# Block diagonals written by ScalarE, the input norm ahead of its slot, and new orders of the units for all rounds but the first four

## The chip, the cores and the metric

One core of a Trainium2 chip runs the kernel; the other cores are idle. The metric is the device time of one execution in microseconds. The median of 3 runs of the kernel before is 1451.22 us (1449.34 to 1452.15).

## What is computed

The input `x` is 128 entries of 32 rows of 512 numbers, with a context of 257 rows for each entry. Three residual layers follow each other, each behind a plain layer norm. Shortened:

```python
x = x + xattn(norm(x), ctx)     # causal self attention (1 head, mask inside an entry), layer norm with gamma, beta;
                                # attention over the entry's 257 context rows, layer norm;
                                # relu(h @ W1 + b1) + h, layer norm, relu
x = x + attn(norm(x))           # 16 heads of 32: q, k, v = x @ W_attn; causal softmax, times a decay matrix; @ W_proj
x = x + ffn(norm(x))            # silu(x @ w1 + b1) * (x @ w2 + b2), layer norm, @ w3 + b3;
                                # the rows named by an index list get gated outputs of 8 experts added
```

Everything is f32 outside; the large products are made of f16 parts.

## The kernel before

The 4096 rows are 32 tiles of 128 rows (4 entries each). A tile passes through some forty units (a unit is a few instructions of one engine: `turn_xn` on TensorE transposes the normed input, `turn_xn` on ScalarE copies it out of PSUM as f16, and so on). Three tiles are in work at once, in three slots (`SLOTN`, tile mod 3), whose buffers and PSUM banks `ps_t[s]` and `ps_a[s]` all units of the tile share; slot 2's buffers lie in one tensor, `last_slot`.

Nothing is scheduled at run time. For each engine a table names the units of one round in order, each with a lag: `(2, "project_k")` in round n is done for tile n - 2. `FIRST` holds for rounds 0 to 3 (with the set-up of the weights, `set_...`), `ORDER` for rounds 4 to 29, `LAST` from round 30 on (with the units of the experts for one tile, `e_...`); `run_pipeline` walks the tables. After the rounds a hardware loop does the expert passes. Between engines there are semaphores only, so an engine stands still when the first instruction of its next unit is not ready, whatever stands behind it.

A product of an activation with a weight has this path: the rows are transposed by TensorE (`turn_...`, four 128x128 f32 transposes), ScalarE copies the result as f16 (`act_h`, the unit of the same name) and once more as f32 (`act_t`, the unit with `_t`), GpSimd makes the remainder `act_l` = `act_t` - `act_h`, TensorE multiplies `act_h` with both parts of the weight (`project_...`, `hidden`, `ffn_in`) and then `act_l` with the high part (the unit with `_l`). Layer norms are on VectorE: `bn_stats`, `bn_aggr`, an addition (`moments`), then GpSimd raises the variance to -0.5 (line 636), then VectorE scales.

The parts that the change touches:
- Lines 1200 and on: `xn_moments` and `turn_xn` (function `xn`) norm the tile's input; they use the slot's `stats`, `mv`, `var` and `rstd`, which the slot's other norms use too.
- Self attention: `self_scores` (VectorE, line 1206) adds the mask, takes the row maximum and scales it into `ntop`; ScalarE exponentiates; `turn_p` transposes the 128x128 weights on TensorE into `ps_a` (line 1770) and ScalarE copies them to `p_t` (line 826); `self_mix` multiplies them with the values.
- Heads: the keys of the 16 heads are laid out block diagonally in `kbd`, so that a matmul serves four heads: `project_k` writes two 32-partition blocks on ScalarE (line 850) and two on VectorE (line 1309). The softmax weights are put block diagonally into `pbd`: `head_weights` on VectorE scales and then transposes four groups of 32 partitions into it (line 1349). TensorE's `head_scores` (line 1814) and `head_mix` (line 1826) read `kbd` and `pbd` as moving operands of 128 columns.
- `ffn_out` on VectorE (lines 1389 and 1391) scales the product and adds `b3`, then adds the residual.
- `Chain` (VectorE): each step of a chain is followed by a wait for its own end.

```python
kbd = of_arena(HALF + 5 * C * D + 16, C * G * HPC * T).rearrange("p (c g h k) -> p c g h k", c=C, g=G, h=HPC)
pbd = of_arena(HALF + 6 * C * D + 16, NH * G * T).rearrange("p (h g q) -> p h g q", h=NH, g=G)
```

## Time and profile before

| | us |
|---|---|
| median of 3 runs | 1451.22 (1449.34 to 1452.15) |
| span of the profiled execution | 1452.8 |
| TensorE (PE) busy | 1365.6, 94% |
| VectorE (DVE) busy | 1128.1, 78% |
| ScalarE (ACT) busy | 601.9, 41% |
| GpSimd (POOL) busy | 526.1, 36% |

The profiled execution is one more execution of the kernel, and all rows below are of it. A matmul's busy time reaches to its modelled end, which lies behind the start of the next; the time that a unit takes in TensorE's queue is read from start to start. PEld is the loading of weights into TensorE, which goes on beside the matmuls. In the lists of instructions a bracket gives the idle time of the engine before the row and what ended it.

### The profile page before, as it was taken

The page shows a single profiled execution, that of the slowest core. Times are in us where ns is not written, and L with a number is a line of the kernel's source. Part 1 is how long each engine was busy: PE and PEld are TensorE (multiplying, and loading weights), DVE is VectorE, ACT ScalarE, POOL GpSimd, SP SyncE. Part 2 cuts the span into 40 slices and gives each one's busy share as a digit, 9 for nine tenths or more (in the row PEclk, how much of TensorE's full clock was granted, in tenths as well). Part 3 has the DMA queues.
Part 4 walks back from the last instruction along what each step waited for, and adds up shares of the span by engine and source line. Part 5 has one row for each costly group of instructions (what it writes and reads, how often), then busy time and mean ns, then how long its engine had stood idle before and what let it go on. Part 6 is the DMA issues. An engine that isn't in the chain of part 4 may idle for free.

```text
span 1452.8 us, 33270 instructions
## 1 busy us (share of the span) xinstructions
PE 1365.6 (94%) x13860; PEld 851.7 (59%) x13861; DVE 1128.1 (78%) x2335; ACT 601.9 (41%) x1147; POOL 526.1 (36%) x545
## 2 busy tenths in 40 slices
PE   7679999999999999999999999999999999998888
PEld 3355566666656666665665656666665666655443
DVE  6787777777787877778778877777778877777776
ACT  2544444443444444343434444444444444443222
POOL 0133333433444333443443333343443433343222
PEclk9899999999999999999999999999999999999899
DMA  9732444433333444433333344443333344434440
GB/s 349 259 131 74 146 146 146 144 123 105 133 112 115 146 146 146 146 137 101 122 130 105 139 146 146 146 142 114 111 138 105 123 146 146 147 134 161 149 161 30
DMA packets 38662, 201.41 MB, mean 139 GB/s; under 512 B 5096, under 2 KB 5992, under 8 KB 28400
## 3 DMA queue, kind: packets, MB, share of 16 engines
q1 hardware_dynamic: 37648, 198.93, 38.3%
q8 instruction: 109, 1.79, 0.5%
q10 hardware_dynamic: 864, 0.36, 0.1%
q14 instruction: 41, 0.34, 0.1%
HBM read 182.24 MB, written 17.04 MB: 137 GB/s over the span
## 4 chain that ended last, share of the span: by engine, by line
PE 70%; DVE 19%; POOL 4%; ACT 4%; issue 3%; DMA 0%; DVEq 0%; POOLq 0%; ACTq 0%; SPq 0%
PE ps_a L1716 11%; PE ps_a L1739 8%; PE ps_t L1739 7%; PE ps_t L1703 6%; PE ps_a L1725 6%; PE ps_a L1751 4%; PE ps_a L1783 4%; POOL rstd L636 4%; PE ps_t L1716 3%; PE ps_v L1716 3%; DVE stats L1178 3%; DVE arena L1309 3%; PE ps_t L1826 2%; PE ps_t L1775 2%; PE ps_t L1751 2%
## 5 line engine op out<-in xcount | busy, mean ns | idle before, releaser
L645 POOL TENSOR_TENSOR act_l<-act_t,act_h 128x512 f16<-128x512 f32 (+1 forms) x176 | 199.5, 1134 | 351.4 <-ACT act_t L789 199.4
L636 POOL TENSOR_TENSOR rstd<-var,mhalf 128x1 f32<-128x1 f32 x224 | 181.8, 812 | 333.7 <-DVE var L1180 328.9
L781 ACT ACTIVATE act_h<-ps_t,scale 128x512 f16<-128x512 f32 (+1 forms) x110 | 70.8, 644 | 206.2 <-PE ps_t L1703 206.2
L645 POOL TENSOR_TENSOR last_slot<-last_slot 128x512 f16<-128x512 f32 x80 | 90.0, 1125 | 156.7 <-ACT last_slot L789 90.8
L1739 PE MATMUL ps_a<-act_h,arena 128*128 128x128 f16 x1408 | 87.6, 221 | 17.3 <-ACT act_h L781 17.3
L1739 PEld LDWEIGHTS ps_a<-act_h,arena 128*128 128x128 f16 x1408 | 81.9, 99 | 28.3 <-ACT act_h L781 21.3
L789 ACT ACTIVATE act_t<-ps_t,scale 128x512 f32<-128x512 f32 (+1 forms) x110 | 70.3, 639 | 49.1 <-PE ps_t L1703 49.1
L1739 PE MATMUL ps_t<-act_h,arena 128*128 128x128 f16 x1408 | 87.0, 221 | 3.3 <-ACT act_h L781 3.3
L1716 PE MATMUL ps_a<-arena,act_h 128*128 128x512 f16 x352 | 83.6, 380 | 1.9 <-ACT act_h L781 1.9
L1309 DVE TENSOR_SCALAR arena<-ps_a,unscale 32x512 f32<-32x512 f32 x64 | 48.2, 753 | 47.0 <-PE ps_a L1751 45.8
L1739 PEld LDWEIGHTS ps_t<-act_h,arena 128*128 128x128 f16 x1408 | 81.4, 99 | 4.9 <-DVE arena L1037 2.4
L1178 DVE BATCH_NORM_STATS2 stats<-rows 128x6 f32<-128x512 f32 x110 | 76.5, 695 | 3.8
L781 ACT ACTIVATE last_slot<-ps_t,scale 128x512 f16<-128x512 f32 (+1 forms) x50 | 32.2, 644 | 89.4 <-PE ps_t L1703 89.4
L1191 DVE SCALAR_TENSOR_TENSOR rows<-rows,rstd,beta 128x512 f32<-128x512 f32 x66 | 50.2, 761 | 22.3 <-POOL rstd L636 22.2
L1716 PE MATMUL ps_a<-w_parts,act_h 128*128 128x512 f16 x264 | 64.2, 379 | 2.0 <-ACT act_h L781 2.0
L1703 PE MATMUL ps_t<-ident,rows 128*128 128x128 f32 x352 | 56.1, 283 | 9.1 <-DVE rows L1184 7.4
L1349 DVE STREAM_TRANSPOSE arena<-rows 32x512 f32<-32x512 f32 x88 | 61.8, 703 | 2.8
L1799 PE MATMUL ps_a<-arena,p_t 128*32 128x512 f32 x512 | 62.6, 607 | 0.0
L1716 PEld LDWEIGHTS ps_a<-arena,act_h 128*128 128x128 f16 x352 | 31.3, 98 | 50.6 <-ACT act_h L781 10.5
L1703 PEld LDWEIGHTS ps_t<-ident,rows 128*128 128x128 f32 x352 | 41.0, 143 | 29.0 <-DVE rows L1184 20.1
L1187 DVE SCALAR_TENSOR_TENSOR rows<-rows,mv,gamma 128x512 f32<-128x512 f32 x66 | 50.3, 762 | 0.0
L1783 PE MATMUL ps_a<-arena,q_t 128*32 128x257 f32 x704 | 44.2, 393 | 4.7 <-ACT q_t L830 4.7
(380 smaller groups left out, 3150.7 us busy)
## 6 DMA issues: line engine op xcount, KB each, us to landing
arena<-in_ctx_t SPq DMA_DIRECT2D x32, 2056.0 KB, 8.4
arena<-in_ctx_n SPq DMA_DIRECT2D x32, 2048.0 KB
ctx_last<-in_ctx_last SPq DMA_DIRECT2D x32, 256.0 KB
arena<-in_ew SPq DMA_DIRECT2D x8, 1024.0 KB, 6.3
x_in<-in_x SPq DMA_DIRECT2D x22, 256.0 KB, 7.3
x_scratch<-rows SPq DMA_DIRECT2D x22, 256.0 KB, 8.8
out<-rows SPq DMA_DIRECT2D x22, 256.0 KB, 2.1
arena<-in_ew SPq DMA_DIRECT2D x8, 512.0 KB, 7.2
```

Of the source, the lines that this page charges most:

```text
L636: nc.gpsimd.tensor_tensor(rstd[s][:], var[s][:], mhalf[:], ALU.pow).then_inc(rstd_ready[s], 1)
L645: nc.gpsimd.tensor_tensor(act_l[s][:, chunks], act_t[s][:, chunks], act_h[s][:, chunks], ALU.subtract).then_inc(act_l_ready[s], 1)
L781: nc.scalar.activation(act_h[s][:, 0:width // P].rearrange("p c r -> p (c r)"), bank[s][:, 0:width], ACT.Copy, scale=scale[:, k:k + 1]).th ...
L789: nc.scalar.activation(act_t[s][:, 0:width // P].rearrange("p c r -> p (c r)"), bank[s][:, 0:width], ACT.Copy, scale=scale[:, k:k + 1]).th ...
L1178: chain(nc.vector.bn_stats(stats[s][:], rows))
L1309: nc.vector.tensor_scalar(kbd[rows, :, :, h, :], ps_a[s][rows, :].rearrange("p (c g k) -> p c g k", c=C, g=G), unscale[rows, K_WATTN:K_WAT ...
L1703: mm = nc.tensor.transpose(out[s][:, c * P:(c + 1) * P], rows[s][:, lo + c * P:lo + (c + 1) * P], ident[:])
L1716: nc.tensor.matmul(bank[s][:], act_h[s][:, c, :], w[:, part, c, lo:lo + D], start=(c == 0 and part == 0), stop=False, skip_group_check=True)
L1725: mm = nc.tensor.matmul(bank[s][:], act_l[s][:, c, :], w[:, 0, c, lo:lo + D], start=False, stop=(c == chunks - 1), skip_group_check=True)
L1739: nc.tensor.matmul(bank[s][:, m * P:(m + 1) * P], w[:, part, c, lo + m * P:lo + (m + 1) * P], act_h[s][:, c, :], start=(m == 0 and c == 0 ...
L1751: mm = nc.tensor.matmul(bank[s][:, m * P:(m + 1) * P], w[:, 0, c, lo + m * P:lo + (m + 1) * P], act_l[s][:, c, :], start=False, stop=(c == ...
L1783: mm = nc.tensor.matmul(ps_a[s][T * g:T * (g + 1), 0:S], q_t[s][:, c, T * g:T * (g + 1)], ctx_t[:, c, g, :], start=(c == 0), stop=(c == C ...
```

## The change

- `kbd` and `pbd` get another order of their axes: the four heads (or groups) of a moving operand no longer lie side by side but 512 words apart, while what is written per head or group is one contiguous piece of 512 words.
- All four key blocks are written by ScalarE, in two units (`project_k`, `project_k2`). VectorE's `project_k` is gone.
- `head_weights` on VectorE does one transposing operation of full width; four copies on ScalarE (`heads_p`, `heads_p2`) put the groups into `pbd`.
- `turn_p` is one block transpose on VectorE (the weights are block diagonal in blocks of 32) in place of TensorE's transpose and ScalarE's copy.
- `b3` is added to the residual by GpSimd (`x2_bias`); `ffn_out` is one operation.
- The input norm has its own small buffers and semaphores (`x_stats`, `x_mv`, `x_var`, `x_rstd`), so that it can be done while the slot still serves tile n - 3. `turn_xn` on VectorE waits for the slot's `turn_x2n`, and TensorE's `project_self` waits for `out_ready` of that tile.
- The scale of the scores is folded into constants; the row maxima are taken negated, so that the one-column scaling after them goes.
- The last step of a chain is not waited for at once, but by its next user (`made_by`).
- `ORDER` and `LAST` are new tables. In `LAST` most units have a lag higher by one, which shifts where its round begins. `FIRST` keeps its sequence, with the units that are gone taken out and the new ones put in.

The core of the diff; `LAST` and `FIRST`, semaphore declarations and renumbered waits are left out:

```diff
 ORDER = {
-    "pe": [(2, "project_q"), (3, "turn_z"), (2, "project_k_l"), (3, "ffn_out"), (3, "ffn_out_l"), (1, "turn_pc"),
-        (2, "project_q_l"), (1, "context_mix"), (2, "head_scores"), (0, "turn_xn"), (2, "project_v"),
-        (0, "project_self"), (0, "project_self_l"), (1, "turn_w"), (2, "project_v_l"), (1, "context_out"),
-        (0, "self_scores"), (1, "context_out_l"), (0, "value_self"), (0, "value_self_l"), (0, "turn_p"),
-        (2, "head_mix"), (0, "self_mix"), (2, "project_out"), (1, "turn_h2"), (2, "project_out_l"), (1, "hidden"),
-        (1, "hidden_l"), (0, "turn_h"), (2, "turn_x2n"), (0, "project_query"), (0, "project_query_l"), (2, "ffn_in"),
-        (0, "context_scores"), (2, "ffn_in_l"), (1, "turn_x1n"), (1, "project_k")],
-    "dve": [(3, "z_norm"), (2, "project_k"), (3, "ffn_out"), (0, "xn_moments"), (1, "context_total"), (0, "turn_xn"),
-        (2, "head_scores"), (1, "context_mix"), (1, "context_scaled"), (2, "head_total"), (0, "project_self"),
-        (2, "head_weights"), (0, "self_scores"), (1, "context_out"), (1, "context_norm"), (0, "self_mix"),
-        (2, "project_out"), (0, "self_norm"), (2, "x2_norm"), (1, "hidden"), (1, "out_norm"), (1, "x1_norm"),
-        (2, "ffn_in"), (0, "context_scores"), (2, "silu")],
-    "act": [(3, "turn_x2n_t"), (2, "turn_x1n"), (3, "ffn_in"), (2, "turn_x1n_t"), (3, "turn_z"), (3, "turn_z_t"),
-        (1, "context_scores"), (2, "project_k"), (1, "turn_pc"), (2, "project_q"), (0, "turn_xn_t"), (0, "turn_xn"),
-        (1, "context_sum"), (2, "head_scores"), (1, "context_scaled"), (0, "project_self"), (1, "turn_w"),
-        (1, "turn_w_t"), (0, "self_scores"), (2, "project_v"), (0, "value_self"), (0, "turn_p"), (2, "head_mix"),
-        (2, "head_mix_t"), (1, "turn_h2"), (1, "turn_h2_t"), (0, "turn_h"), (0, "turn_h_t"), (2, "turn_x2n"),
-        (0, "project_query")],
-    "pool": [(3, "silu"), (3, "turn_z"), (0, "xn_moments"), (0, "turn_xn"), (2, "head_scores"), (1, "turn_w"),
-        (1, "context_out"), (2, "head_mix"), (0, "self_mix"), (1, "turn_h2"), (2, "project_out"), (0, "turn_h"),
-        (1, "hidden"), (2, "turn_x2n"), (1, "out_norm"), (1, "turn_x1n")],
+    "pe": [(2, "project_v"), (1, "turn_pc"), (2, "project_q"), (3, "turn_z"), (2, "project_k_l"), (1, "context_mix"),
+        (2, "project_q_l"), (3, "ffn_out"), (3, "ffn_out_l"), (0, "turn_xn"), (2, "head_scores"),
+        (2, "project_v_l"), (1, "turn_w"), (0, "project_self"), (0, "project_self_l"), (1, "context_out"),
+        (1, "context_out_l"), (0, "value_self"), (0, "self_scores"), (0, "value_self_l"), (2, "head_mix"),
+        (1, "turn_h2"), (0, "self_mix"), (2, "project_out"), (2, "project_out_l"), (1, "hidden"), (0, "turn_h"),
+        (1, "hidden_l"), (0, "project_query"), (0, "project_query_l"), (2, "turn_x2n"), (0, "context_scores"),
+        (2, "ffn_in"), (1, "turn_x1n"), (2, "ffn_in_l"), (1, "project_k")],
+    "dve": [(0, "xn_moments"), (3, "ffn_in"), (3, "silu"), (3, "z_norm"), (1, "context_total"), (0, "turn_xn"),
+        (1, "context_mix"), (1, "context_scaled"), (3, "ffn_out"), (2, "head_scores"), (2, "head_total"),
+        (0, "project_self"), (2, "head_weights"), (1, "context_out"), (0, "self_scores"), (1, "context_norm"),
+        (0, "turn_p"), (0, "self_mix"), (0, "self_norm"), (2, "project_out"), (1, "hidden"), (2, "x2_norm"),
+        (1, "out_norm"), (1, "x1_norm"), (0, "context_scores")],
+    "act": [(2, "turn_h2"), (2, "turn_h2_t"), (1, "turn_h_t"), (1, "turn_h"), (1, "project_query"), (3, "turn_x2n"),
+        (3, "turn_x2n_t"), (2, "turn_x1n"), (3, "ffn_in"), (2, "turn_x1n_t"), (1, "context_scores"),
+        (1, "turn_pc"), (3, "turn_z_t"), (2, "project_k2"), (3, "turn_z"), (2, "project_k"), (2, "project_q"),
+        (1, "context_sum"), (1, "context_scaled"), (0, "turn_xn_t"), (0, "turn_xn"), (2, "head_scores"),
+        (1, "turn_w_t"), (1, "turn_w"), (0, "project_self"), (2, "heads_p"), (2, "project_v"), (2, "heads_p2"),
+        (0, "self_scores"), (0, "value_self"), (2, "head_mix"), (2, "head_mix_t")],
+    "pool": [(2, "turn_x1n"), (0, "xn_moments"), (3, "turn_z"), (3, "x2_bias"), (0, "turn_xn"), (2, "head_scores"),
+        (1, "turn_w"), (1, "context_out"), (2, "head_mix"), (0, "self_mix"), (1, "turn_h2"), (2, "project_out"),
+        (0, "turn_h"), (1, "hidden"), (1, "out_norm"), (2, "turn_x2n"), (2, "silu")],
 }
...
-            kbd = of_arena(HALF + 5 * C * D + 16, C * G * HPC * T).rearrange("p (c g h k) -> p c g h k", c=C, g=G, h=HPC)
-            pbd = of_arena(HALF + 6 * C * D + 16, NH * G * T).rearrange("p (h g q) -> p h g q", h=NH, g=G)
+            kbd = of_arena(HALF + 5 * C * D + 16, C * G * HPC * T).rearrange("p (h c g k) -> p h c g k", c=C, g=G, h=HPC)
+            pbd = of_arena(HALF + 6 * C * D + 16, NH * G * T).rearrange("p (g h q) -> p g h q", h=NH, g=G)
...
+                def x2_bias(s, r, tile):
+                    pool.wait_ge(rows_ready[s], 5 * r + 4)
+                    pool.wait_ge(x2_stored[s], 16 * r + 32)
+                    if tile == 0:
+                        pool.wait_ge(late_loaded, 16 * 7)
+                    nc.gpsimd.tensor_tensor(rows3[s][:], rows3[s][:], b3[:], ALU.add).then_inc(x2_biased, 1)
...
+                def key_blocks(heads):
+                    def unit(s, r, tile):
+                        act.wait_ge(k_done[s], r + 1)
+                        if tile == 0:
+                            act.wait_ge(consts_ready, 4)
+                        else:
+                            act.wait_ge(scored[(s - 1) % SLOTN], 3 * (r - (s == 0)) + 3)
+                        for h in heads:
+                            mine = slice(HD * h, HD * (h + 1))
+                            nc.scalar.activation(kbd[mine, h, :, :, :].rearrange("p c g k -> p (c g k)"),
+                                                 ps_a[s][mine, :], ACT.Copy,
+                                                 scale=unscale[mine, K_WATTN:K_WATTN + 1]).then_inc(k_ready, 1)
+                    return unit
+
+                def weight_blocks(groups):
+                    def unit(s, r, tile):
+                        act.wait_ge(heads_turned, tile + 1)
+                        if tile == 0:
+                            act.wait_ge(consts_ready, 5)
+                        else:
+                            act.wait_ge(y_done[(s - 1) % SLOTN], r + (s > 0))
+                        for g in groups:
+                            mine = slice(T * g, T * (g + 1))
+                            nc.scalar.copy(pbd[mine, g, :, :].rearrange("p h q -> p (h q)"), rows3[s][mine, :]
+                                           ).then_inc(pbd_ready, 1)
+                    return unit
 
...
                     def __call__(self, ins):
+                        self.last(ins)
+                        dve.wait_ge(dve_step[self.s], steps_in_all * self.r + steps_before[self.unit] + self.count)
+
+                    def last(self, ins):
                         self.count += 1
...
                     dve.wait_ge(x_loaded[s], 16 * r + 16)
-                    moments(chain, s, x_in[s][:], 1e-5)
-                    chain.end()
+                    nc.vector.bn_stats(x_stats[s][:], x_in[s][:]).then_inc(x_step, 1)
+                    dve.wait_ge(x_step, 2 * tile + 1)
+                    nc.vector.bn_aggr(x_mv[s][:], x_stats[s][:]).then_inc(x_step, 1)
+                    dve.wait_ge(x_step, 2 * tile + 2)
+                    nc.vector.tensor_scalar(x_var[s][:], x_mv[s][:, 1:2], 1e-5, None, ALU.add).then_inc(x_var_ready, 1)
 
                 def xn(s, r, tile):
-                    plain_norm(s, r, 1, rows1[s][:], x_in[s][:]).then_inc(rows_ready[s], 1)
+                    dve.wait_ge(x_rstd_ready, tile + 1)
+                    if tile >= SLOTN:
+                        dve.wait_ge(turned[s], 7 * r - 1)
+                    nc.vector.tensor_scalar(rows1[s][:], x_in[s][:], x_mv[s][:, 0:1], x_rstd[s][:], ALU.subtract,
+                                            ALU.mult).then_inc(x_rows, 1)
...
-                                            ).then_inc(ntop_ready[s], 1)
+                    nc.vector.reduce_max(ntop[s][:], rows3[s][:, 0:P], AX.X, negate=True).then_inc(ntop_ready[s], 1)
+                    chain.end()
+
+                def turn_p(s, r, tile):
+                    chain = Chain("turn_p", s, r)
+                    dve.wait_ge(p_ready[s], 3 * r + 1)
+                    nc.vector.transpose(p_t[s][:, 0:P], p_n[s][:, 0:P]).then_inc(p_t_ready[s], 1)
+                    chain.last(nc.vector.reciprocal(inv[s][:, 0:1], total[s][:, 0:1]))
                     chain.end()
...
-                def project_k(s, r, tile):
-                    dve.wait_ge(k_done[s], r + 1)
-                    if tile == 0:
-                        dve.wait_ge(consts_ready, 4)
-                    else:
-                        dve.wait_ge(scored[(s - 1) % SLOTN], 3 * (r - (s == 0)) + 3)
-                    for h in (2, 3):
-                        rows = slice(HD * h, HD * (h + 1))
-                        nc.vector.tensor_scalar(kbd[rows, :, :, h, :],
-                                                ps_a[s][rows, :].rearrange("p (c g k) -> p c g k", c=C, g=G),
-                                                unscale[rows, K_WATTN:K_WATTN + 1], None, ALU.mult
-                                                ).then_inc(k_ready[s], 1)
+                    plain_norm(s, r, 4, rows1[s][:], rows2[s][:]).then_inc(rows_ready[s], 1)
 
...
                     chain(nc.vector.tensor_tensor(by_head(rows1[s][:]), sc, per_head(inv[s][:]), ALU.mult))
-                    for g in range(G):
-                        rows = slice(T * g, T * (g + 1))
-                        nc.vector.transpose(pbd[rows, :, g, :], by_head(rows1[s][rows, :])).then_inc(pbd_ready[s], 1)
+                    nc.vector.transpose(sc, by_head(rows1[s][:])).then_inc(heads_turned, 1)
                     chain.end()
...
-                    chain = Chain("ffn_out", s, r)
-                    chain(nc.vector.scalar_tensor_tensor(rows2[s][:], ps_a[s][:], unscale[:, K_W3:K_W3 + 1], b3[:],
-                                                         ALU.mult, ALU.add))
-                    nc.vector.tensor_tensor(rows2[s][:], rows2[s][:], rows3[s][:], ALU.add).then_inc(out_ready[s], 1)
-                    chain.end()
+                    dve.wait_ge(x2_biased, tile + 1)
+                    nc.vector.scalar_tensor_tensor(rows2[s][:], ps_a[s][:], unscale[:, K_W3:K_W3 + 1], rows3[s][:],
+                                                   ALU.mult, ALU.add).then_inc(out_ready[s], 1)
...
+                def project_self(s, r, tile):
+                    pe.wait_ge(act_h_ready[s], 8 * r + 1)
+                    if tile >= SLOTN:
+                        pe.wait_ge(out_ready[s], r)
+                    high_t(ps_a, 1, wqk)(s, r, tile)
```

## Rows read from the trace of the kernel before

**Rows 1.** The page, busy time by engine, and TensorE's granted clock in 40 slices
```profile
PE 1365.6 (94%) x13860; PEld 851.7 (59%) x13861; DVE 1128.1 (78%) x2335; ACT 601.9 (41%) x1147; POOL 526.1 (36%) x545
...
PEclk9899999999999999999999999999999999999899
```

**Rows 2.** Windows: stretch, its length, busy us of the engines, clock, DMA share, GB/s
```profile
727.22:767.86 40.64, 39.46 (x431) 25.17 (x427) 32.13 (x67) 17.41 (x34) 16.02 (x17) 1.00 0.37 131
...
1283.91:1327.50 43.59, 39.76 (x425) 25.37 (x425) 34.15 (x67) 17.39 (x35) 15.59 (x17) 1.00 0.34 122
1327.50:1423.60 96.10, 83.67 (x602) 45.26 (x602) 69.80 (x152) 27.34 (x55) 26.01 (x29) 0.95 0.49 173
```

**Rows 3.** Chain that ended last (start, length, what), the pieces of `context_scores`
```profile
226.45 1.87 PE ps_a L1783 x32
...
1242.29 1.87 PE ps_a L1783 x32
...
1284.11 1.94 PE ps_a L1783 x32
```

**Rows 4.** The same chain, three units of one round
```profile
720.07 1.79 PE ps_t L1739 x32
...
729.00 1.73 PE ps_v L1716 x8
...
733.84 0.86 PE ps_v L1725 x4
```

**Rows 5.** TensorE's instructions in order of time, one round: start, length, line
```profile
716.73 0.60 PE L1703 MATMUL ps_t<-ident,rows 128*128 128x128 f32 x4
718.11 1.96 PE L1739 MATMUL ps_a<-act_h,arena 128*128 128x128 f16 x32 [0.78 <-ACT act_h L781]
...
722.81 1.03 PE L1716 MATMUL ps_a<-w_parts,last_slot 128*128 128x512 f16 x4
723.83 0.60 PE L1725 MATMUL ps_a<-w_parts,last_slot 128*128 128x512 f16 x2
...
740.43 0.27 PE L1770 MATMUL ps_a<-ident,p_n 128*128 128x128 f32 x1
740.63 1.08 PE L1826 MATMUL ps_t<-arena,v_n 128*32 128x128 f32 x32
...
749.49 0.66 PE L1703 MATMUL ps_t<-ident,rows 128*128 128x128 f32 x4 [0.33 <-DVE rows L1184]
```

**Rows 6.** The chain where it is on VectorE: a key block, and `ffn_out`'s second operation
```profile
723.01 0.75 DVE arena L1309
...
725.37 0.69 DVE last_slot L1391
```

**Rows 7.** Groups of instructions by form: count, busy us and mean ns, idle time before
```profile
L645 POOL TENSOR_TENSOR act_l<-act_t,act_h 128x512 f16<-128x512 f32 x154 | 184.8, 1200 | 303.7 <-ACT act_t L789 151.6 <-ACT act_h L781 77.3 <-ACT act_t L808 31.9
...
L1349 DVE STREAM_TRANSPOSE arena<-rows 32x512 f32<-32x512 f32 x88 | 61.8, 703 | 2.8
...
L850 ACT ACTIVATE arena<-ps_a,unscale 32x512 f32<-32x512 f32 x64 | 43.1, 673 | 1.2 <-PE ps_a L1751 0.3
...
L826 ACT COPY p_t<-ps_a 128x128 f32<-128x128 f32 x32 | 8.3, 260 | 2.5 <-PE ps_a L1770 2.5
```

**Rows 8.** ScalarE in order of time: two full-width copies of one turn, two key blocks
```profile
704.34 0.69 ACT L781 ACTIVATE act_h<-ps_t,scale 128x512 f16<-128x512 f32 x1 [1.92 <-PE ps_t L1703]
...
704.92 0.68 ACT L789 ACTIVATE act_t<-ps_t,scale 128x512 f32<-128x512 f32 x1
...
723.30 1.37 ACT L850 ACTIVATE arena<-ps_a,unscale 32x512 f32<-32x512 f32 x2
```

**Rows 9.** VectorE and GpSimd in order of time: the chain of `hidden`, two powers
```profile
708.72 0.74 DVE L1282 SCALAR_TENSOR_TENSOR rows<-ps_a,unscale,b 128x512 f32<-128x512 f32 x1
...
711.24 0.74 DVE L1187 SCALAR_TENSOR_TENSOR rows<-rows,mv,gamma 128x512 f32<-128x512 f32 x1
...
711.40 0.99 POOL L636 TENSOR_TENSOR rstd<-var,mhalf 128x1 f32<-128x1 f32 x1 [0.20 <-DVE var L1180]
...
715.18 0.55 POOL L636 TENSOR_TENSOR rstd<-var,mhalf 128x1 f32<-128x1 f32 x1 [0.19 <-DVE var L1180]
```

257 lines of the change are left out of this document (126 added, 131 removed), and 8 rows, old and new, of the table FIRST.

## The prediction

> **What bounds the kernel now.** I read the page's busy table first: TensorE is busy 94% of the span, VectorE 78%, ScalarE 41%, GpSimd 36%, and the clock row shows full speed but for the two ends [rows 1]. So TensorE's queue sets the time, and the question is how much of it is waiting that the "busy" number hides, because one matmul's tail covers the start of the next. For that the windows by stage come next [rows 2]: a steady round is 40.6 us with TensorE 39.5 busy; the last two rounds of the main loop and the expert tail (1327.5 to 1423.6) are looser, the tail with 83.7 busy in 96.1. The chain of waits gives the exact period, from the start of the first matmul of `context_scores` in one round to that in the next: 1242.29 less 226.45 is 1015.84 over 25 rounds, 40.63 us; the next step is 41.82 [rows 3]. All 26 rounds of `ORDER` have that period, whichever slot they use, so a wait found in one round is there 26 times.
>
> Then TensorE's own order of one round, start against start. The chain gives what a unit takes when nothing holds it: 1.79 us for 32 matmuls of 128 columns, 1.73 for 8 of 512, 0.86 for 4 of 512 [rows 4]. Summed over the 36 units that stay, such prices come to 37.9 us; the round is 40.63, of which 0.20 is `turn_p` (740.43 to 740.63, with the switch to the next unit) [rows 5]. So about 2.5 us of a round are waits or switches between kinds of matmul. The large ones: `project_k` starts at 718.11, though `turn_x1n` before it had streamed by 717.17, which is 0.94 (that turn goes to ScalarE and back with nothing put between); `turn_x2n` starts at 749.49, 0.55 after its predecessor's 0.44 were over. `ffn_out_l` comes 1.02 after `ffn_out`, where 0.86 would do, and three more like that (`turn_xn`, `hidden_l`, `project_query_l`) bring the small ones to 0.43 [rows 5]. What is left, some 0.5, is switching that any order has.
>
> In the middle of the round the chain leaves TensorE for VectorE: two key blocks, `ffn_out`'s two operations, then the norm of the input, up to `turn_xn` [rows 6]. That is the path that the change cuts.
>
> **The change part by part.** VectorE loses per tile two key blocks (2 x 0.75 = 1.5), one of `ffn_out`'s operations (0.69) [rows 6], three of four head transposes (3 x 0.70 = 2.1; one of full width replaces the four, and I take it at the row's 0.70, since the partitions run side by side) [rows 7], and two one-column scalings, small beside these. It gains one 128x128 block transpose; no row shows one, the nearest is 0.70 for 512 columns, so up to 0.70, taken as 0.25 by the columns. Net about 4.1 us off 32.1 per round. None of it is worth anything by itself: VectorE is idle for 8 us of a round [rows 2].
>
> TensorE loses `turn_p`, 0.20. The transposed weights now come off VectorE 0.3 us after the exponential instead of after a turn on TensorE and a 0.26 copy on ScalarE [rows 7], and `self_mix` stands late enough in the new order to find them ready.
>
> ScalarE gains two key blocks at 0.67 and four copies of 32x512. No row shows the copies; the nearest, full-width operations, start 0.58 apart (704.34, 704.92) [rows 8], and the two key blocks now take 1.37 together, 0.70 apart. So 0.58 to 0.70 each, taken as 0.65; +3.9 us less the 0.26 copy, on 17.4 per round. What is queued behind them matters. Behind the key blocks stand `project_q`, the row sum, its scaling and both copies of `turn_xn`, for which `project_self` waits. From the end of `project_k_l` at 4.9 us into the round (round start: `project_v`) I get: key blocks and `turn_z` to 7.7, `project_q` 8.2, the sum to 9.4, two small VectorE steps 0.35, scaling, then `turn_xn_t` and `turn_xn`, done at 11.5 to 11.9. TensorE reaches `project_self` at 11.8. Cost 0 to 0.15. Behind the weight copies, which wait for VectorE's `head_weights` (done at about 17.3), stand `project_v`, `self_scores` and `value_self`; the copies end at 20.3 to 20.7, and TensorE wants them for `head_mix` at 20.6. Cost 0 to 0.15.
>
> GpSimd gains `x2_bias`, one addition of 128x512; the nearest row is its remainders at 1.20, on an engine with 16.0 of 40.6 us busy [rows 2, 7]. It runs at about 7.5 to 8.7, where VectorE waits for `context_mix`; `ffn_out` needs it at 9.8. Nothing, by this cover; up to 1.2 without it. In the trace a one-column power takes 0.99 us where VectorE's two-input scaling started just before it (711.24, 711.40), and 0.55 where none runs (715.18) [rows 9]: one engine does hold the other up. The Trainium skill says so too (SBUF — State Buffer, "Who interferes with whom"): a VectorE instruction with two SBUF inputs and a GpSimd instruction that reads SBUF exclude each other, whichever came first. By that rule the new addition could hold a VectorE operation for its whole length; in the trace it is GpSimd that waits.
>
> The explicit waits: `turn_xn` on VectorE now stands before `context_mix`; it needs the previous owner's `turn_x2n`, ten microseconds old. `project_self` waits for `out_ready`, at about 10.5, and is asked for at 11.8. The waits dropped at the ends of chains are worth about 0.1 each on VectorE, off the path. `store_x2` lands before `x2_bias` by about 2.8 us.
>
> The order is what moves the round. `turn_x1n` now has `ffn_in_l` behind it (0.86), so its wait falls from 0.94 to 0.08: -0.86. `turn_x2n` stands after `project_query_l`, so the old 0.55 goes, but two new waits stand there. First, ScalarE makes `turn_h_t` before `turn_h`, and only `hidden_l` (0.86) covers that: 0.2 to reach ScalarE, 0.58, 0.69, less 0.86, is +0.66 ahead of `project_query`. Second, `x2_norm` now stands behind `hidden` on VectorE, whose chain is five dependent steps from 708.72 to 711.98, 3.26 us [rows 9]; with 0.2 to reach it and 0.55 for the norm, less its overlap, `turn_x2n` can start 4.0 after `hidden_l` ends. TensorE has 0.66 + 1.79 + 0.89 = 3.34 till then: +0.63. `context_out` waits 0.1 for `turn_w`, which stands behind the heads' exponential. The small waits of 0.43 go, since what they wait for comes earlier.
> Round: 40.63 - 0.20 - 0.86 - 0.55 - 0.43 + 0.66 + 0.63 + 0.12 = 40.0, and with half of the ScalarE costs 40.05: -0.58. Times 26: -15.
>
> The first four rounds keep their sequence; they gain `turn_p` and relief of VectorE: -1, between -4 and +3. The last two rounds take 41.8 and 43.6, and the tail has 12 us without a matmul [rows 2, 3]; the new order spreads the expert units over it anew. I have not walked that stretch: -4, between -12 and +6.
>
> The sum is against the profiled execution: 1452.8 - 15 - 1 - 4 = 1432.8. It lies 1.6 over the median of 1451.22, so 1431.
>
> **The rivals.**
> 1. *The waits go altogether.* If ScalarE and VectorE are quicker than my walk where it counts (the 0.66 and 0.63 shrink to the ScalarE round trip), the round nears 37.9 + 0.5 of switches; say 39.0, -42, and with the tail 1400 to 1418. For: VectorE has the idle time. Against: the 3.26 chain is made of measured steps.
> 2. *ScalarE becomes the chain.* If a 32x512 instruction costs its 0.70 and something more in the queue, `project_self`, `context_out` and `head_mix` each wait 0.15 more: the round is 40.5 and the time 1443 to 1450. For: key blocks are 0.70 apart now. This takes in the case that the edits do nothing because the hidden chain has simply replaced the old one.
> 3. *Slower: TensorE reads gapped operands.* The new layouts put the four heads or groups of a moving operand 512 words apart, where they were 128 words in one piece, for 64 matmuls per tile. No row shows such a read. If they stream at half speed, `head_mix` (1.08 with its tail, 1.0 net [rows 5]) and `head_scores`, as many matmuls of the same width, double: +2.0 x 32 = +64, less the 20 above, 1495; it decides from 0.3 us more on each, above which the change is slower. Against: runs of 32 words stay whole, and these are f32 matmuls, slow per column already.
>
> **How the numbers follow.** Forecast 0.52 (1420 to 1440), waits go 0.17, ScalarE chain 0.19, gapped operands or an equal loss in the tail 0.12. Range 1406 to 1450: it holds the forecast, the second rival, most of the first, and the unknown tail. 0.2% (3 us) is about what a measurement of this kernel can tell from no change. Faster: 0.52 + 0.17 + 0.12 of the second rival = 0.81; same 0.07; slower 0.12.
>
> **What would show it.** In the trace after: a period near 40.0 between `context_scores` starts; `project_k` right behind `ffn_in_l`; a wait of about 0.6 at `project_query` for ScalarE and one like it at `turn_x2n` for VectorE; `head_scores` and `head_mix` still 1.0; ScalarE near 21 us per round and VectorE near 28. A period under 39.3 would say that I overrate the chain behind `hidden`; over 40.6, that ScalarE or the operands bite.

## The result: slower, 1513.1 against 1451.7 us

The changed kernel takes 1513.12 us (median of 4 runs, 1510.67 to 1517.99), the kernel before in the same comparison 1451.68 (1449.34 to 1452.31): ratio 1.0436, 95% interval 1.0414 to 1.0458. The forecast was 1431, in a range that ended at 1450.

The page of after, busy time by engine and the chain that ended last:
```profile
PE 1372.6 (91%) x13828; PEld 848.8 (56%) x13829; DVE 1098.2 (72%) x2112; ACT 720.6 (48%) x1307; POOL 550.2 (36%) x577
...
DVE 27%; PE 23%; ACT 18%; issue 13%; POOL 7%; DVEq 0%; POOLq 0%
```
A steady round of after as a window, and the next one (columns as in [rows 2]):
```profile
710.00:752.89 42.89, 39.63 (x426) 25.04 (x425) 31.86 (x61) 21.17 (x40) 16.65 (x17) 1.00 0.35 124
752.89:795.78 42.89, 39.64 (x426) 25.04 (x425) 31.85 (x61) 21.17 (x40) 16.64 (x17) 1.00 0.35 124
```
The round is 42.89 us, where it was 40.63 [rows 2, 3], with TensorE's granted clock at 1.00 in both. VectorE executes 61 instructions where it had 67 and is busy for 31.86 us; the forecast had 28. It does less work in nearly the same busy time, so single instructions must have become longer. The row of a kernel's first `turn_pc` on TensorE, those of the following rounds and the span divide the time:

| us | before | after | difference |
|---|---|---|---|
| up to the first `turn_pc` | 69.25 | 67.99 | -1.3 |
| next three steps (first rounds) | 126.8 | 130.4 | +3.6 |
| next 25 steps | 1015.8 | 1070.4 | +54.6 |
| from there to the end | 240.9 | 247.4 | +6.5 |

Of the 63.4 us between the two spans, 54.6 stand in the steady rounds. VectorE and GpSimd of after in order of time, in the middle of one round (lines 1231, 1331 and 1223 are here `self_norm`, the second operation of `hidden`, and `x1_norm`; line 644 is GpSimd's power, line 657 its remainder; the row of 754.19 is `z_norm`, on 256 columns; line 1277 is `self_mix`, and line 1226 ends the chain of `hidden`):
```profile
733.42 1.16 POOL L657 TENSOR_TENSOR last_slot<-last_slot 128x512 f16<-128x512 f32 x1 [2.87 <-ACT last_slot L905]
733.44 0.75 DVE L1277 SCALAR_TENSOR_TENSOR rows<-ps_t,inv,rows 128x512 f32<-128x512 f32 x1 [1.71 <-PE ps_t L1810]
...
735.40 0.98 POOL L644 TENSOR_TENSOR rstd<-var,mhalf 128x1 f32<-128x1 f32 x1 [0.82 <-DVE var L1219]
736.36 1.15 POOL L657 TENSOR_TENSOR act_l<-act_t,act_h 128x512 f16<-128x512 f32 x1
736.42 1.64 DVE L1231 SCALAR_TENSOR_TENSOR rows<-rows,rstd,beta 128x512 f32<-128x512 f32 x1 [0.44 <-POOL rstd L644]
...
739.77 0.74 DVE L1329 SCALAR_TENSOR_TENSOR rows<-ps_a,unscale,b 128x512 f32<-128x512 f32 x1
...
740.45 1.16 POOL L657 TENSOR_TENSOR act_l<-act_t,act_h 128x512 f16<-128x512 f32 x1
740.55 1.61 DVE L1331 SCALAR_TENSOR_TENSOR rows<-rows 128x512 f32<-128x512 f32 x1
...
743.21 0.74 DVE L1226 SCALAR_TENSOR_TENSOR rows<-rows,mv,gamma 128x512 f32<-128x512 f32 x1
...
747.17 0.55 POOL L644 TENSOR_TENSOR rstd<-var,mhalf 128x1 f32<-128x1 f32 x1 [2.73 <-DVE var L1219]
747.68 1.15 POOL L657 TENSOR_TENSOR last_slot<-last_slot 128x512 f16<-128x512 f32 x1
747.75 1.37 DVE L1223 TENSOR_SCALAR rows<-rows,mv,rstd 128x512 f32<-128x512 f32 x1 [0.66 <-POOL rstd L644]
...
754.19 1.37 DVE L1231 SCALAR_TENSOR_TENSOR last_slot<-last_slot,rstd,ln_b 128x256 f32<-128x256 f32 x1 [0.44 <-POOL rstd L644]
```
Three times the same picture: a remainder starts on GpSimd, 0.06 to 0.10 us later an operation of VectorE, and this one takes 1.37 to 1.64 us where it takes 0.55 to 0.75 when alone; such an operation is called held below. It ends 0.29 to 0.55 behind the remainder's end. In two of the three, GpSimd's power released VectorE's operation, and the remainder stood right behind the power in GpSimd's queue, with its inputs ready; VectorE always comes a moment too late. `z_norm` is the fourth of the kind: a remainder starts at 754.12, and 1.37 us stand where 0.48 would do. Two more operations of the heads are held in every round (1.42 and 0.91 for 0.69), so that the six have 4.5 us too much. Not every operation is held: `self_mix` (line 1277) reads one operand in PSUM and one in SBUF, starts 0.02 behind a remainder (733.42, 733.44) and keeps its 0.75, and `bn_stats` with its single input takes 0.69 behind a remainder as elsewhere.

The chain of `hidden`, from the start of line 1329 to the end of line 1226, takes 4.18 us (739.77 to 743.95), where the prediction counted 3.26 from [rows 9].

In the kernel before, the remainder behind the same power (`self_mix`, then `turn_h2`) had to wait for ScalarE, and VectorE's 0.75 (line 1191) fell into the gap:
```profile
741.06 0.99 POOL L636 TENSOR_TENSOR rstd<-var,mhalf 128x1 f32<-128x1 f32 x1 [4.69 <-DVE var L1180]
742.16 0.75 DVE L1191 SCALAR_TENSOR_TENSOR rows<-rows,rstd,beta 128x512 f32<-128x512 f32 x1 [0.51 <-POOL rstd L636]
743.19 1.16 POOL L645 TENSOR_TENSOR act_l<-act_t,act_h 128x512 f16<-128x512 f32 x1 [1.14 <-ACT act_t L875]
```
Groups of after from 600 to 1000 us, a little over nine rounds. The first mixes held and free operations of one line; the last is the heads' subtraction:
```profile
L1231 DVE SCALAR_TENSOR_TENSOR rows<-rows,rstd,beta 128x512 f32<-128x512 f32 x20 | 21.2, 1059 | 3.5 <-POOL rstd L644 3.1
...
L1331 DVE SCALAR_TENSOR_TENSOR rows<-rows 128x512 f32<-128x512 f32 x7 | 11.3, 1609 | 0.2
...
L1361 DVE TENSOR_TENSOR rows<-rows,top 128x512 f32<-128x512 f32 x6 | 8.5, 1421 | 0.2
```
TensorE's waits of after in the same stretch (sum, how many, longest):
```profile
PE ps_t L1730 <- DVE rows L1223: 11.0, 12, 1.5
PE ps_t L1730 <- DVE last_slot L1223: 5.5, 6, 1.5
PE ps_t L1772 <- ACT act_h L800: 3.5, 7, 0.5
PE ps_a L1749 <- ACT act_h L823: 2.9, 6, 0.5
PE ps_a L1730 <- DVE rows L1231: 2.8, 7, 0.4
```
Per round that is 1.48 at `turn_x2n`, 0.35 at `turn_x1n`, 0.40 at `turn_h`, 0.48 at `context_out` and 0.49 at `project_query`.

### The profile page after: what moved, and what is told of

Its sections match the earlier page's. It is cut to its first block, busy times and chain, and to the rows that moved or that the text cites. A ratio compares the mean times of both kernels' runs of the same rounds, so it can differ in the third digit from the quotient of the medians.

```text
span 1516.2 us, 33367 instructions
## 1 busy us (share of the span) xinstructions
PE 1372.6 (91%) x13828; PEld 848.8 (56%) x13829; DVE 1098.2 (72%) x2112; ACT 720.6 (48%) x1307; POOL 550.2 (36%) x577
## 4 chain that ended last, share of the span: by engine, by line
DVE 27%; PE 23%; ACT 18%; issue 13%; POOL 7%; DVEq 0%; POOLq 0%
POOL rstd L644 5%; PE ps_a L1772 4%; ACT arena L866 4%; PE ps_t L1772 4%; ACT arena L880 3%; PE ps_v L1749 3%; DVE stats L1217 3%; PE ps_t L1861 2%; DVE rows L1231 2%; DVE rows L1331 2%; PE ps_a L1758 2%; PE ps_t L1730 2%; DVE rows L1223 2%; PE ps_a L1784 2%; DVE rows L1361 2%
## 5 line engine op out<-in xcount | busy, mean ns | idle before, releaser
L644 POOL TENSOR_TENSOR rstd<-var,mhalf 128x1 f32<-128x1 f32 x192 | 155.4, 810 | 477.6 <-DVE var L1219 477.6
L657 POOL TENSOR_TENSOR act_l<-act_t,act_h 128x512 f16<-128x512 f32 (+1 forms) x176 | 195.3, 1110 | 253.2 <-ACT act_h L800 134.1
L866 ACT ACTIVATE arena<-ps_a,unscale 32x512 f32<-32x512 f32 x128 | 86.5, 675 | 17.6 <-PE ps_a L1784 15.8
L1772 PE MATMUL ps_a<-act_h,arena 128*128 128x128 f16 x1408 | 87.5, 221 | 1.6 <-ACT act_h L800 1.6
L1730 PE MATMUL ps_t<-ident,rows 128*128 128x128 f32 x264 | 44.0, 290 | 40.9 <-DVE rows L1223 37.6
L1231 DVE SCALAR_TENSOR_TENSOR rows<-rows,rstd,beta 128x512 f32<-128x512 f32 x66 | 67.1, 1017 | 13.2 <-POOL rstd L644 11.8
L880 ACT COPY arena<-rows 32x512 f32<-32x512 f32 x88 | 54.2, 616 | 46.2 <-DVE rows L1377 44.5
L1730 PEld LDWEIGHTS ps_t<-ident,rows 128*128 128x128 f32 x264 | 28.6, 143 | 61.2 <-DVE rows L1223 53.0
L1297 DVE SCALAR_TENSOR_TENSOR v_n<-ctx_last,p_n,ps_a 128x512 f32<-128x512 f32 x22 | 16.4, 747 | 58.8 <-PE ps_a L1834 58.8
L800 ACT ACTIVATE last_slot<-ps_t,scale 128x512 f16<-128x512 f32 (+1 forms) x50 | 32.1, 642 | 49.2 <-PE ps_t L1730 48.9
L808 ACT ACTIVATE act_t<-ps_a,scale 128x512 f32<-128x512 f32 x22 | 15.1, 685 | 74.3 <-PE ps_a L1730 74.3
```

The costliest lines, as they stand in the source:

```text
L644: nc.gpsimd.tensor_tensor(rstd[s][:], var[s][:], mhalf[:], ALU.pow).then_inc(rstd_ready[s], 1)
L657: nc.gpsimd.tensor_tensor(act_l[s][:, chunks], act_t[s][:, chunks], act_h[s][:, chunks], ALU.subtract).then_inc(act_l_ready[s], 1)
L800: nc.scalar.activation(act_h[s][:, 0:width // P].rearrange("p c r -> p (c r)"), bank[s][:, 0:width], ACT.Copy, scale=scale[:, k:k + 1]).th ...
L808: nc.scalar.activation(act_t[s][:, 0:width // P].rearrange("p c r -> p (c r)"), bank[s][:, 0:width], ACT.Copy, scale=scale[:, k:k + 1]).th ...
L866: nc.scalar.activation(kbd[mine, h, :, :, :].rearrange("p c g k -> p (c g k)"), ps_a[s][mine, :], ACT.Copy, scale=unscale[mine, K_WATTN:K_ ...
L880: nc.scalar.copy(pbd[mine, g, :, :].rearrange("p h q -> p (h q)"), rows3[s][mine, :]).then_inc(pbd_ready, 1)
```

## Experiments

The theory: GpSimd's remainders, which read two operands in SBUF, hold VectorE's operations that start just behind them, and the new order makes such pairs. The rivals: the new sequence has longer dependent chains in itself; `x2_bias`, the new GpSimd operation, is the collider; GpSimd is simply busy too long; ScalarE's added work is the bound.

### The old sequence with the new units

Only `ORDER` is changed; `LAST` stays the new one.

```diff
 ORDER = {
-    (the new sequence)
+    (the sequence of before: turn_p on VectorE behind context_out, project_k2 behind project_k,
+     heads_p and heads_p2 ahead of self_scores on ScalarE, x2_bias behind turn_z on GpSimd)
```


> All edits of the units stay (block diagonals by ScalarE, block transpose, x2_bias, own buffers of the input norm); only ORDER gets back the sequence of the kernel before, with the new units put in (heads_p and heads_p2 ahead of self_scores on ScalarE, turn_p behind context_out on VectorE); LAST stays the new one. Theory, contention by order (the new order sets GpSimd's remainders just ahead of VectorE's operations with two SBUF inputs on the path through hidden, x2_norm and x1_norm, which then take 1.4 to 1.6 us in place of 0.55 to 0.7): the period of a round falls from 42.9 to 40.6 or less, the time to 1440 to 1457. Rival, the load of ScalarE or the operands with gaps: these edits are all still in, so the period stays above 42 and the time above 1495. The rival that the order is bad by its own dependences, without contention, expects the same as the theory here.

Measured: 1493.73 us, ratio 1.0292 (1.0265 to 1.0320), a miss. The round is 42.08 on average. No 128x512 operation is held (`hidden`'s is back at 692 ns), but VectorE has a new wait (600 to 1000 us):
```profile
DVE rows L1415 <- POOL rows L672: 33.0, 6, 6.3
```
`ffn_out` waits up to 6.3 us for `x2_bias`, and that for the store of x2, which in this sequence has not landed:
```profile
706.23 1.26 POOL L672 TENSOR_TENSOR rows<-rows,b 128x512 f32<-128x512 f32 x1 [1.37 <-DMA x_scratch<-rows]
```
So the sequence isn't the whole cause, and the parts have costs of their own in another sequence.

### Remainders that read nothing

```diff
-                        nc.gpsimd.tensor_tensor(act_l[s][:, chunks], act_t[s][:, chunks], act_h[s][:, chunks],
-                                                ALU.subtract).then_inc(act_l_ready[s], 1)
+                        nc.gpsimd.memset(act_l[s][:, chunks], 0.0).then_inc(act_l_ready[s], 1)
```


> The kernel after, but GpSimd's remainders (act_l = act_t - act_h) are a fill with zeros of the same tile, behind the same waits: GpSimd writes and no longer reads SBUF there. The low part of the products is left out by this. Theory, contention: VectorE's long operations (1.4 to 1.6 us) fall back to 0.55 to 0.75, the period to 40 to 41, the time to 1435 to 1465. Rival, the order's own dependences (hidden ahead of x2_norm, both copies of turn_h) or ScalarE's load: VectorE's durations may fall, but the period stays above 42 and the time above 1490.

Measured: 1435.75 us, 0.9909 (0.9892 to 0.9925); the round is 40.18. The operations with two inputs in SBUF are back at their lengths: the group of `hidden`'s is
```profile
L1330 DVE SCALAR_TENSOR_TENSOR rows<-rows 128x512 f32<-128x512 f32 x7 | 4.8, 692 | 0.2
```
and TensorE's waits in ten rounds are
```profile
PE ps_t L1729 <- DVE rows L1222: 3.3, 7, 0.5
PE ps_t L1771 <- ACT act_h L799: 3.0, 6, 0.5
PE ps_t L1771 <- ACT last_slot L799: 2.0, 4, 0.5
PE ps_t L1860 <- ACT arena L879: 1.9, 10, 0.2
```
One kind stays held a little, by the fill: `x1_norm`, a TENSOR_SCALAR, takes 0.72 where it takes 0.54 alone.
```profile
754.02 0.52 POOL L657 MEMSET act_l<- 128x512 f16 x1
754.11 0.72 DVE L1222 TENSOR_SCALAR rows<-rows,mv,rstd 128x512 f32<-128x512 f32 x1 [0.66 <-POOL rstd L644]
```
The fills take 77 us off the changed kernel. The same edit on the kernel before:

> The control for the one above: the kernel before with the same zero fill in place of the remainders, so the low part of the products is left out here too. Theory, contention: the order of before suffers little, so 0 to 15 us faster than before, 1436 to 1451. If the fill itself makes the kernel quick for another reason (a shorter GpSimd unit that TensorE waits for), this one gains as much as the one above, 40 us or more.

Measured: 1443.61 us, 0.9955 (0.9938 to 0.9971), the round 40.50. The old order had next to nothing to lose by the remainders, 6 us; the new one had 77. Like for like, both with fills, the changed kernel is 7.9 us faster than the one before, 0.32 per round. But a fill is also shorter (0.52) than a remainder (1.16). So the fill was issued twice per unit:

> The kernel after, with each remainder on GpSimd replaced by two fills of the same tile one after the other, so that the unit takes about 1.1 us as the remainder does, but reads nothing in SBUF. The low part of the products is left out. Theory, contention of reads: the period stays where one fill had it, 40.2 to 40.6, and the time at 1433 to 1450. Rival, the length of GpSimd's units in the chain (TensorE's _l units wait for them): the period goes back above 42, the time above 1490.

Measured: 1437.23 us, 0.9923 (0.9904 to 0.9942), the round 40.18 again, with GpSimd as busy as in after (157.3 us of 400, after 155.7):
```profile
L663 POOL MEMSET act_l<- 128x512 f16 x47 | 25.8, 548 | 2.7
L661 POOL MEMSET act_l<- 128x512 f16 x47 | 24.6, 523 | 38.8 <-ACT act_t L910 21.0 <-ACT act_h L805 17.8
```
So it isn't GpSimd's load: what costs the time goes away when its instruction no longer reads SBUF.

### x2_bias undone

Shortened to its two ends:
```diff
-    ..., (3, "x2_bias"), ...
+                    nc.vector.tensor_tensor(rows2[s][:], rows2[s][:], rows3[s][:], ALU.add)   # ffn_out as before
```


> The kernel after with x2_bias alone taken back (ffn_out is two operations on VectorE). Theory, contention by GpSimd's remainders: they are all there, so the time is 1500 to 1530. Rival, the added GpSimd operation is what collides with VectorE or delays the queue: the period falls below 41.5, the time below 1480.

Measured: 1507.80 us, 1.0400 (1.0382 to 1.0419), the round 42.89 as in after. `x2_bias` isn't the collider. VectorE has its 0.69 for `ffn_out`'s second operation again, but the heads' subtraction, which follows, now starts a full microsecond behind the remainder that held it and takes 0.70 in place of 1.42: the two cancel, and TensorE's waits are the same as in after. So the operation that `x2_bias` saved was lost to a hold just behind it. The holds of `self_norm`, `hidden` and `x1_norm` are all still there (1.64, 1.61, 1.37).

### Moving the pairs apart by the order

One move, GpSimd's `(1, "turn_h2")` from behind `(0, "self_mix")` to ahead of it:

> The kernel after with one pair swapped in GpSimd's list of ORDER: the remainder of turn_h2 goes ahead of the power of self_mix. In the trace of after that remainder starts 0.06 us ahead of VectorE's self_norm and holds it for 0.9. Theory, contention: self_norm takes 0.75 again, but its power comes 0.2 to 0.3 later; turn_h starts 0.6 earlier; the period falls by 0 to 0.7, the time by 0 to 18 (1495 to 1513). Rival, dependences: the power comes later and nothing is won, 1513 to 1520.

Measured: 1498.34 us, 1.0334 (1.0304 to 1.0364), the round 42.31. `self_norm` is free, and `turn_h` no longer waits. With five moves more (GpSimd's `turn_h` ahead of `project_out`, and `turn_x2n` ahead of `out_norm`; ScalarE's two copies of `turn_w` ahead of the heads' exponential, and `turn_h` ahead of `turn_h_t`):

> The kernel after, all work kept, with six moves in ORDER that take GpSimd's remainders away from VectorE's two-input operations: on GpSimd turn_h2 ahead of self_mix, turn_h ahead of project_out, turn_x2n ahead of out_norm; on ScalarE turn_w and turn_w_t ahead of head_scores, and turn_h ahead of turn_h_t. Theory, contention by order: the period falls from 42.9 to between 40.2 and 41.3, the time to 1440 to 1472. Rival, dependences and ScalarE's load: no move but that of turn_h helps, the period stays above 42, the time above 1490.

Measured: 1479.78 us, 1.0207 (1.0189 to 1.0225), the round 41.76, less of a gain than the theory had and more than the rival. `self_norm` and `x1_norm` are free (749 and 544 ns), `hidden`'s and the heads' operation still held, by other remainders than before:
```profile
L1328 DVE SCALAR_TENSOR_TENSOR rows<-rows 128x512 f32<-128x512 f32 x7 | 9.6, 1373 | 0.2
...
L1358 DVE TENSOR_TENSOR rows<-rows,top 128x512 f32<-128x512 f32 x6 | 8.5, 1422 | 0.2
```

### Shorter remainders

Every remainder in two instructions of half the columns; nothing is left out:
```diff
-                        chunks = slice(0, width // P)
-                        nc.gpsimd.tensor_tensor(act_l[s][:, chunks], act_t[s][:, chunks], act_h[s][:, chunks],
-                                                ALU.subtract).then_inc(act_l_ready[s], 1)
+                        half = width // P // 2
+                        for part in range(2):
+                            chunks = slice(part * half, (part + 1) * half)
+                            sub = nc.gpsimd.tensor_tensor(act_l[s][:, chunks], act_t[s][:, chunks],
+                                                          act_h[s][:, chunks], ALU.subtract)
+                        sub.then_inc(act_l_ready[s], 1)
```


> The changed kernel; each of GpSimd's remainders is issued as two instructions of half the columns (about 0.6 us each by the measured 0.67 for 128x256, against 1.16 for 128x512). Nothing is left out, the order is the changed one. If VectorE's two-input operation waits only for the end of the one GpSimd instruction that had started before it, the held operations lose about 0.25 to 0.35 us each instead of 0.65 to 0.9: hidden's second operation near 1.05 instead of 1.61 in mid-run, the period 41.0 to 41.6 instead of 42.89, the time 1455 to 1480. Rival: if the two engines don't take turns between instructions, the second half holds it as well, and GpSimd is 0.18 us longer per remainder: period 42.9 or more, time 1507 to 1525.

Measured: 1464.16 us, 1.0090 (1.0069 to 1.0110), the round 41.08: 49 us less than after, by an edit that adds instructions and leaves nothing out. `hidden` in order of time:
```profile
760.43 1.75 POOL L659 TENSOR_TENSOR last_slot<-last_slot 128x256 f16<-128x256 f32 x2
760.53 1.12 DVE L1334 SCALAR_TENSOR_TENSOR rows<-rows 128x512 f32<-128x512 f32 x1
```
The operation takes 1.12, not 1.61: it gets its turn between the halves, and now the second half seems to wait for it (1.75 for two, where two take 1.29 to 1.38 in the kernel before in halves, below).

> The changed kernel with each of GpSimd's remainders in four instructions of a quarter of the columns; halves brought the period from 42.89 to 41.08 and the time to 1464.2. From 1.16 and 0.67 for 512 and 256 columns, 128 columns should take about 0.43 (estimate), 1.7 for a remainder. If a VectorE operation waits only for the end of the one instruction that had started before it, each hold shrinks again, hidden's second operation from 1.12 (halves) to 0.85 to 1.0, the period to 40.5 to 40.9, the time to 1446 to 1460. Rival: the remainders are now 0.55 longer, and TensorE waits for them (project_query_l already waits 0.2 with halves); the gain is spent: period 41.0 to 41.6, 1461 to 1480.

Measured: 1481.37 us, 1.0210 (1.0182 to 1.0239), the round 41.55; the rival held, with a time 1 us above its range. The holds did shrink (777 ns for `hidden`'s), but a remainder is now four times 488 ns, 1.95, and TensorE waits for it:
```profile
PE ps_a L1764 <- POOL act_l L662: 2.8, 13, 0.3
PE ps_t L1867 <- ACT arena L886: 2.5, 9, 0.3
...
PE ps_a L1764 <- POOL last_slot L662: 1.5, 7, 0.3
```
Halves together with moves:

> The changed kernel with the six moves of the run that moved the operations apart (period 41.76) and the remainders in halves. What was still held there were hidden's second operation (1.37), head_scores (1.42), head_weights (1.20) and z_norm (1.37). If halves shorten each hold to 0.3, the period is 40.7 to 41.2 and the time 1445 to 1463. Rival (no turns between instructions): period 41.8 or more, 1480 to 1490.

Measured: 1471.64 us, 1.0144 (1.0127 to 1.0161), the round 41.39, a miss. `self_norm` and `x1_norm` are free here, but the remainder of `turn_h` comes later, and `project_query_l` waits 0.5 for it where it waited 0.2. Four moves of the six:

> As the changed kernel with halves, and of the six moves only four: GpSimd's remainder of turn_h2 before the power of self_mix, and on ScalarE both copies of turn_w before the exponential of the heads, and turn_h before turn_h_t. The two powers of project_out and out_norm stay before the remainders, so x2's and x1's rstd come a remainder earlier and x1_norm is held a little. If a hold costs only 0.3 with halves, this is as fast as or faster than all six moves: period 40.6 to 41.1, 1443 to 1462. Rival: the holds of x1_norm and hidden outweigh the earlier powers, and it is slower than all six moves by 5 to 15 us.

Measured: 1468.13 us, 1.0126 (1.0101 to 1.0151), the round 41.31, a miss too. With halves the moves cost more than the holds that they avoid. Halves alone on the kernel before:

> The kernel before, with each of GpSimd's remainders in two instructions of half the columns; nothing else is changed. With all its remainders replaced by fills the kernel before gained 6 us (period 40.50 instead of 40.63), so its order meets hardly any hold. If splitting helps only where operations are held, this gains 0 to 4 us: 1446 to 1451, period 40.5 to 40.65. Rival: shorter GpSimd instructions help in some other way (the remainder or the powers behind it come sooner), then this gains 6 us or more too; or the 0.18 per remainder costs, and it is slower by 2 to 8 us.

Measured: 1457.72 us, 1.0050 (1.0034 to 1.0067), the round 40.88: 7.9 us slower, where a small gain was expected. Where next to nothing is held, splitting costs (682 ns per half, 1.36 for 1.19) and gains nothing.

### What the parts cost in the old sequence

The old sequence again, `x2_bias` undone:

> The sequence of the kernel before in ORDER with the new units, as in e1_old_order, but x2_bias is taken back: ffn_out is again two operations on VectorE, and nothing waits for the landed store of x2. Theory: what e1_old_order lost is the wait of ffn_out for x2_bias, which waits for a store that lands late in that order; without it the period is 40.2 to 40.7 and the time 1440 to 1453. Rival, ScalarE's added load or the other edits cost in themselves: the period stays above 41.5, the time above 1475.

Measured: 1472.74 us, 1.0161 (1.0141 to 1.0181), a miss, though 21 us less than with `x2_bias`. The round is 41.39, and no 128x512 operation is held. TensorE waits once per round for the copy of `turn_pc`, which stands behind the four key blocks on ScalarE:
```profile
PE ps_a L1833 <- ACT p_t L852: 9.8, 10, 1.0
```
So that copy was put ahead of the key blocks:

> The old sequence of units with the new units put in and x2_bias undone (1472.7 us, period 41.39), with one move: on ScalarE the copy of turn_pc now stands before the four key blocks instead of behind them. The theory that these two added key blocks (0.70 each) are what the old sequence pays for says: context_mix no longer waits for that copy (9.8 us in ten rounds before), the period falls by 0.6 to 0.9, to 40.5 to 40.8, and the time to 1449 to 1458. Rival: the key blocks are then late for head_scores by as much, or VectorE is the one that is late; then the period stays at 41.1 to 41.5 and the time at 1465 to 1477.

Measured: 1481.13 us, 1.0208 (1.0191 to 1.0225), the round 41.66, slower than theory and rival had it. That wait is gone, and `head_scores` waits instead, for `project_q` behind the same key blocks:
```profile
PE ps_a L1848 <- ACT q_t L883: 7.8, 7, 1.1
```
Place doesn't help, so the work itself was taken away: two of the four blocks back on VectorE.
```diff
-        (1, "context_scores"), (2, "project_k"), (2, "project_k2"), (1, "turn_pc"), ...    # ScalarE
+        (1, "context_scores"), (2, "project_k"), (1, "turn_pc"), ...
-    "dve": [(3, "z_norm"), (3, "ffn_out"), ...
+    "dve": [(3, "z_norm"), (2, "project_k2"), (3, "ffn_out"), ...
```


> The old sequence of units with the new units, x2_bias undone (1472.7, period 41.39), and two of the four key blocks given back to VectorE, at its old place in the queue. Moving all four behind turn_pc's copy only moved the wait, from context_mix to head_scores, and the period was 41.66. If ScalarE's two added key blocks (1.38 us in a stretch where TensorE waits for ScalarE either way) are what the old sequence pays for, both waits go and the period is 40.5 to 40.8, the time 1446 to 1457. Rival: the loss comes from elsewhere (the copies of the weights, VectorE's later ffn_out), and the period stays at 41.2 or more, 1465 to 1475.

Measured: 1448.11 us, 0.9987 (0.9977 to 0.9997), a round of 40.48:
```profile
700.00:740.48 40.48, 39.30 (x436) 25.04 (x429) 30.16 (x63) 19.70 (x38) 15.93 (x16) 1.00 0.37 131
```
So ScalarE's two added key blocks are the 0.9 us per round that the old sequence loses. Last, the first rounds. In after, TensorE waits in two of them for VectorE's transpose, which stands behind `project_out` (waits of after, 100 to 200 us):
```profile
PE ps_t L1810 <- DVE p_t L1268: 3.5, 2, 1.8
PE ps_t L1738 <- DVE rows L1245: 2.3, 1, 2.3
```
The kernel with quarters, that transpose earlier in the first rounds, and `x2_bias` undone:

> As the run with quarters, and two edits for the first rounds, whose steps 2 and 3 are 44.8 and 45.5 where the kernel before has 43.5 and 42.8: VectorE's transpose of the weights (turn_p) stands before project_out's operations in the first rounds (self_mix waited 1.8 for it twice), and x2_bias is undone (in the first rounds it stood on GpSimd ahead of the power for the input norm, and turn_xn waited 2.3 for that once). If these two are the first rounds' loss, steps 2 and 3 sum to 85 to 87.5 instead of 90.3, and the time is 3 to 6 us below the run with quarters: 1441 to 1457. Rival: the steps stay at 89 to 90, since other waits take their place, and the time is within 1.5 us of the run with quarters.

Measured: 1488.26 us, 1.0258 (1.0241 to 1.0275), a miss: 7 us slower than quarters alone. The second and third step fell by 6.4 us together (46.68 and 48.26 to 45.40 and 43.17), to a sum of 88.6, short of the 85 to 87.5 expected. The steady round rose by 0.6 to 42.14: TensorE's waits for remainders (line 1764, here 1763) doubled, from 4.3 to 8.6 us in ten rounds. Why undoing `x2_bias` does this with quarters and nothing without them was not followed up. Then the transpose's place alone, on the version that is level with before:

```diff
 FIRST "dve": ... (0, "self_scores"), (0, "set_08"), (1, "context_norm"),
-             (2, "project_out"), (1, "set_19"), (0, "turn_p"), (0, "self_mix"), ...
+             (0, "turn_p"), (2, "project_out"), (1, "set_19"), (0, "self_mix"), ...
```


> The old sequence with two key blocks given back to VectorE and x2_bias undone (1448.1 us, against 1449.8 before), and one move in the first rounds: VectorE's transpose of the weights stands before project_out's operations, since self_mix waited 1.8 for it in two of these rounds (3.5 us). If that wait is on the path, steps 2 and 3 (44.76 and 44.11) lose 2 to 3.5 us together and the time is 1444.5 to 1446.5, ratio 0.9960 to 0.9980. Rival: project_out's operations, now 0.3 later, hold up the next unit instead, and the time stays within 1 us of 1448.1.

Measured: 1446.78 us, 0.9975 (0.9964 to 0.9985); the two steps fell by 1.45 and 1.48 to 43.31 and 42.63, the one ahead of them by 1.9. The time is 1.3 below that of the run above, less than its own 12 runs are apart (1443.90 to 1449.11), so what the move is worth isn't settled. Against the kernel before, this version is 3.7 us faster: the changed layouts, transposes, input norm and chains, in the old sequence, without `x2_bias` and with the key blocks shared as they were.

## Why the prediction was wrong, step by step

- *What bounds the kernel, and the walk of the round*: right in the main. With the remainders' reads gone the round is 40.18 where the sum had 40.0 to 40.05, and the time 1435.75 where it had 1431. But the fills give the kernel before 6 us too; against it with fills the change is worth 7.9 us and 0.32 per round, where 20 and 0.58 were forecast. Wait by wait: `project_query` 0.49 (sum 0.66), `turn_x2n` 0.47 (0.63), `head_mix` 0.19 (0 to 0.15), `context_out` none (0.1); `project_k` no longer waits. Over the spans, the fills' kernel against before: +3.2 up to the end of the first rounds (sum -1), -13.1 in 25 steps (-15 for 26), -8.9 for the end (-4).
- *Slips in the sum*: 0.2 + 0.58 + 0.69 - 0.86 is 0.61 and not 0.66, with which the wait behind it is 4.0 less 3.29, 0.71 and not 0.63; and half of two costs of 0 to 0.15 is 0.15, where 0.05 was added. By its own terms the round is 40.18 and the time 1434.5. That the fills' round is 40.18 to the digit is luck, since the single waits differ.
- *The failed step* is the sentence "in the trace it is GpSimd that waits", by which the collision of the two engines was put at nothing and made no rival, so that the walk of the new order used VectorE's lengths of the old one: the chain of `hidden` at 3.26, which measured 4.18 (and 3.26 again with fills), and the wait at `turn_x2n` at 0.63, which measured 1.48. [Rows 9] show a power held by 0.44 behind VectorE's operation; by the rows above, who is held depends on who starts second, and a reordering changes just that. The missing term is 2.71 us per round (42.89 less 40.18), 67.7 over 25 steps, and some 15 more in the end (247.4 against 232.0 with fills). It accounts for the whole difference, and more: without it the change is faster than before. The Trainium skill (SBUF — State Buffer, "Who interferes with whom") states the rule: the ports that the two engines share are an exclusive lock, and the order of issue decides who is blocked. The runs agree, with 1.61 behind a remainder of 1.16 and 1.12 behind half of one. It also says that a GpSimd instruction that only writes leaves two-input operations alone; by the two runs with fills (692 ns) that holds as well. I cited that rule and weighed it only for `x2_bias`. The halves, which leave nothing out, brought back 49 of the 61 us.
- *The trace of before had one already.* Not only GpSimd waits in it: in every steady round `z_norm`'s first operation, on 256 columns, starts behind a remainder and takes 0.61; with fills it takes 0.47.
```profile
759.72 1.16 POOL L645 TENSOR_TENSOR act_l<-act_t,act_h 128x512 f16<-128x512 f32 x1 [3.35 <-ACT act_t L789]
760.54 0.61 DVE L1187 SCALAR_TENSOR_TENSOR v_n<-v_n,mv,ln_g 128x256 f32<-128x256 f32 x1
```
- *It could have been read beforehand.* In the new tables a power is followed on GpSimd by a remainder in `self_mix`, `turn_h2`; `project_out`, `turn_h`; and `out_norm`, `turn_x2n`, and by the new sequence of TensorE the remainder's inputs are early; in the old ones the first two pairs stand as well, but the inputs come late (for `turn_h2` 1.14 behind the power, above), and `out_norm` is followed by `turn_x1n`. Its price, worked out afterwards from rows at hand: 1.20 [rows 7] less 0.1 by which VectorE comes later, for three operations on the path, 3.3 us per round where 2.7 were measured.
- *`x2_bias` at no cost*: right in the new sequence (in the steady rounds neither VectorE nor TensorE waits for it, and undoing it leaves the round at 42.89, since the heads' hold then goes), 21 us in the old one, where the store lands later. In the first rounds it stands ahead of the input norm's power; undoing it took 2.25 off the third step (45.50 to 43.25).
- *ScalarE's added work, 0 to 0.15 at three places*: about right in the new sequence, where only `head_mix` shows it. The prices were good: key blocks 0.675, copies of 32x512 0.616 (I took 0.65). In the old sequence the same key blocks cost 0.9 per round.
- *VectorE's prices*: the transpose of full width 0.711 (taken 0.70), the 128x128 one 0.311 (taken 0.25). The 28 us of busy time came with fills (27.6).
- *First four rounds at -1*: wrong in sign, +2.3 (-1.3 and +3.6), though inside the stated -4 to +3. They gained waits of 1.8, twice, for the transpose behind `project_out`, and one of 2.3 behind `x2_bias`.
- *Rivals*: none held. Gapped operands had the right direction and, at 1495, the nearest time, which is luck, for the reason is refuted: `head_scores` and `head_mix` still take 1.08 (1.01 to the next start), and with them in place the kernel runs at 1436 with fills.
```profile
719.05 1.08 PE L1849 MATMUL ps_a<-arena,last_slot 128*32 128x128 f32 x32
...
730.87 1.08 PE L1861 MATMUL ps_t<-arena,last_slot 128*32 128x128 f32 x32
```

What stays open: the end of the program lost 6.5 us against before, of which fills return all and more; which operations of the expert units are held there was not taken apart. That the new sequence loses nothing else was shown only with the remainders' work left out. No order that keeps whole remainders and frees all the operations was found; the six moves brought back 33 us of the 61. How the 2.71 divides among the single holds isn't known either.

## What to carry to other kernels

Where, as here, VectorE and GpSimd hold each other up, a new order is a new set of collisions: list for each long GpSimd instruction that reads SBUF which VectorE operation with two SBUF inputs (or TENSOR_SCALAR from SBUF to SBUF) can start just behind it, and look first at pairs that one semaphore starts together (a power, behind it a remainder, and the operation that the power releases). Busy time that stays (31.9 for 32.1 us) while the instruction count falls (61 for 67) is the sign of it; a write-only stand-in of the same length tells it from load. Splitting the holder in two pays where something is held (49 us here) and costs where next to nothing is (8 us), and work moved to an idle engine is free only in a sequence that leaves it free at that spot.

## What the runs showed of the hardware

- A TENSOR_SCALAR of f32 from SBUF to SBUF, with one tensor input and two one-column operands, is held like a two-input one, 0.54 alone and 1.37 behind a remainder, and a little by a fill too (0.72). An operation with one input in PSUM and one in SBUF is not held (0.75 for `self_mix` behind a remainder), nor is `bn_stats` with one input in SBUF (0.69 in both).
- A remainder of 128x512 takes 1.16 with nothing beside it, 128x256 0.67, 128x128 0.43 (0.49 on average in the kernel with quarters), so splitting in four makes 1.95 of 1.16.
- Moving operands in runs of 32 words, 512 words apart, stream as fast as 128 words in one piece: 1.08 for 32 f32 matmuls in both.
